# The first half of the node update by plain float32 matmuls on the weights as loaded

## What is computed

```python
h = maximum(layernorm(x), 0)
# layer 0: three kinds of edges (hh, oo, ho), logits from gathered rows
feat = concatenate([h[src], h[dst]], axis=1)
logit = relu(feat @ W_kind + b_kind) @ W_a + b_a
alpha = softmax of logit over the edges of one dst
z = segment_sum(alpha * h[src], dst)
nf2 = concatenate([h, z], axis=1)             # 512 x 2048
h_new = relu(nf2[:128] @ W_hn + b_hn)          # node update
o_new = relu(nf2[128:] @ W_on + b_on)
x = x + concatenate([h_new, o_new])
# layer 1
x = x + normalized_adjacency @ (maximum(layernorm(x), 0) @ W.T + b)
```

## Time and profile before

| | |
|---|---|
| times of 3 runs | 653.9, 653.91, 651.59 us, median 653.9 |
| profiled execution | 651.15 us, span 649.0 us, mean granted clock 0.939 |
| PE, PEld | 556.4 us (86%), 412.9 us (64%) |
| DVE, ACT, POOL | 454.9 us (70%), 307.4 us (47%), 176.3 us (27%) |
| DMA | 140.51 MB, mean 216 GB/s |
| chain that ended last | PE 57%, DVE 20%, DMA 11%, ACT 6% |

### The profile page before, as it was taken

One profiled execution on the slowest core, in us unless ns is written; L12 is line 12 of the kernel. 1 busy time (PEld: TensorE's weight loads), 2 busy tenths in 40 slices (PEclk: granted clock), 3 DMA queues, 4 the chain that ended last, 5 costly groups with the idle time before them and its releaser, 6 DMA issues.

```text
span 649.0 us, 8205 instructions
## 1 busy us (share of the span) xinstructions
PE 556.4 (86%) x2376; PEld 412.9 (64%) x2377; DVE 454.9 (70%) x958; ACT 307.4 (47%) x485; POOL 176.3 (27%) x165
## 2 busy tenths in 40 slices
PE   0799999999839998959899997558949999779987
PEld 0688777777617776647576775224738778667865
DVE  6715256786985879988989887486795289783252
ACT  2623312214088996556565755399743182322200
POOL 2000300165464664555647642200030000000000
PEclk9999999999968999989889999688968899979999
DMA  8334453499999999999999997943355075121021
GB/s 330 122 135 163 151 202 124 144 259 380 316 308 356 330 343 325 303 321 333 284 361 327 349 348 262 232 136 103 127 213 208 16 249 198 41 88 42 0 82 48
DMA packets 55973, 140.51 MB, mean 216 GB/s; under 512 B 6274, under 2 KB 6402, under 8 KB 55938
## 3 DMA queue, kind: packets, MB, share of 16 engines
q0 software_dynamic: 20624, 74.98, 37.5%
q1 hardware_dynamic: 27072, 50.34, 22.0%
q10 hardware_dynamic: 8242, 14.75, 6.1%
HBM read 123.27 MB, written 16.78 MB: 216 GB/s over the span
## 4 chain that ended last, share of the span: by engine, by line
PE 57%; DVE 20%; DMA 11%; ACT 6%; issue 4%; POOL 1%; ACTq 0%; DVEq 0%; POOLq 0%
PE ps L638 35%; DMA gath<-tab_b,tabl_i 8%; PE ps L624 6%; PE ps L588 5%; DVE gath L893 4%; PE ps L797 3%; ACT onehot L482 3%; PE ps L769 3%; DVE ring_l L868 2%; PE ps L782 2%; DVE gath L888 2%; DMA gath<-tab_a,tabl_i 2%; DVE onehot L910 2%; DVE logit_d L932 1%; DVE logit_d L1021 1%
## 5 line engine op out<-in xcount | busy, mean ns | idle before, releaser
L638 PE MATMUL ps<-ring_h,actT_h 128*128 128x512 f32 x520 | 226.0, 435 | 28.2 <-ACT stage L453 16.4
L638 PE MATMUL ps<-ring_h,actT_l 128*128 128x512 f32 x520 | 206.4, 397 | 0.0
L638 PE MATMUL ps<-ring_l,actT_h 128*128 128x512 f32 x520 | 206.2, 397 | 0.0
L435 ACT CAST ring_h<-raw 128x512 fp32r<-128x512 f32 x176 | 105.0, 616 | 118.4 <-PE ps L638 82.8
L482 ACT ACTIVATE onehot<-onehot,lgs 128x512 bf16<-128x512 bf16 x192 | 124.6, 712 | 69.4 <-DVE onehot L910 55.3
L868 DVE TENSOR_TENSOR ring_l<-raw,ring_h 128x512 fp32r<-128x512 f32 x176 | 116.8, 685 | 43.2 <-ACT ring_h L435 42.9
L638 PEld LDWEIGHTS ps<-ring_h,actT_h 128*128 128x128 f32 x520 | 99.9, 192 | 60.8 <-ACT stage L453 18.3
L638 PEld LDWEIGHTS ps<-ring_h,actT_l 128*128 128x128 f32 x520 | 99.7, 192 | 22.4
L638 PEld LDWEIGHTS ps<-ring_l,actT_h 128*128 128x128 f32 x520 | 100.0, 192 | 20.3
L293 POOL DMA_INDIRECT gath<-tab_a,tabl_i x64 | 71.0, 1109 | 150.2 <-DVE gath L893 77.0
L588 PE MATMUL ps<-onehot 128*128 128x512 bf16 x292 | 83.8, 397 | 20.8 <-ACT onehot L482 17.8
(11 more groups left out here) (162 smaller groups left out, 505.1 us busy)
## 6 DMA issues: line engine op xcount, KB each, us to landing
raw<-in_L_gnn_W_ho_dram SPq DMA_DIRECT2D x32, 256.0 KB
raw<-in_L_gnn_W_oo_dram SPq DMA_DIRECT2D x32, 256.0 KB
raw<-in_L_gnn_W_hh_dram SPq DMA_DIRECT2D x32, 256.0 KB
raw<-in_L_gnn_W_on_dram SPq DMA_DIRECT2D x32, 256.0 KB
raw<-in_L_gnn_W_hn_dram SPq DMA_DIRECT2D x32, 256.0 KB
tab_a<-stage ACTq DMA_DIRECT2D x24, 256.0 KB
tab_b<-stage ACTq DMA_DIRECT2D x24, 256.0 KB
raw<-in_L_gnn_W_dram SPq DMA_DIRECT2D x16, 256.0 KB
```

Of the source, the lines that this page charges most:

```text
L435: nc.scalar.copy(ring_h[:, k, :], raw[:, k % RAW, :]).then_inc(s_high, 1)
L638: mm = nc.tensor.matmul(ps[:, first + m, :], w, v, start=(k == 0 and i == 0), stop=(k == KT - 1 and i == 2))
```

## The change

In chunks 12 to 15 PE no longer takes the three float32r passes. It runs one plain float32 matmul for each block and step, with `actT` as weights and `raw[k]` as loaded (`node_chunk`). So ACT has no `round_w` and DVE no `low_w` for these 32 steps. `actT` is the sum of the two parts of `h`; DVE writes it over `actT_l`, slice j at its place (11, j+2), after PE has finished step (11,j), the last reader of that slice of `actT_l`. A slice of `raw` is free for the next load only when PE has read it: the loads of chunks 13 to 16 wait for PE's step one chunk earlier, where they waited for DVE's `low_w`. The counters of later chunks are renumbered by `nth_split`.

```diff
+        actT = sb("actT", [P, KT, N], F32, over="actT_l")
...
                 for k in range(KT):
+                    if q == CH_EDGE:
+                        sp.wait_ge(s_low, q * KT + k + 1)
+                    elif q <= CH_NODE:
+                        sp.wait_ge(s_slot, KT + (q - 1) * KT + k + 1)
+                    else:
+                        sp.wait_ge(s_low, nth_split(q) * KT + k + 1)
                     load(w, row, n, q, k)
...
-                    if q * KT + k + AHEAD < (CH_EDGE + 4) * KT:
+                    if q * KT + k + AHEAD < CH_EDGE * KT:
                         rounds(q * KT + k + AHEAD, q * KT + k + AHEAD + 1)
...
+            def node_chunk(q, ms, bank_free, before):
+
+                for k in range(KT):
+                    before(k)
+                    pe.wait_ge(s_raw[k], 16 * q + 16)
+                    pe.wait_ge(s_whole, k + 1)
+                    for m in ms:
+                        if k == 0 and bank_free:
+                            bank_free(m)
+                        mm = nc.tensor.matmul(ps[:, NM + m, :], actT[:, k, m * P:(m + 1) * P], raw[:, k, :], start=(k == 0), stop=(k == KT - 1))
+                    mm.then_inc(s_slot, 1)
...
-                chunk(q + c, NM, ms, free, before=lambda k: last_sums(q + c, k))
+                node_chunk(q + c, ms, free, before=lambda k: last_sums(q + c, k))
...
-                    if q1 < CH_EDGE + 4:
+                    if q1 < CH_EDGE:
                         low_w(q1, k1)
...
+                    j = (q - CH_EDGE + 1) * KT + k - 2
+                    if 0 <= j < KT:
+                        dve.wait_ge(s_slot, KT + (CH_EDGE - 1) * KT + j + 1)
+                        nc.vector.tensor_tensor(actT[:, j, :], f32(actT_h[:, j, :]), f32(actT_l[:, j, :]), ALU.add).then_inc(s_whole, 1)
```

More of the change, by code:

```diff
@@ L162, in gnn_kernel @@
         s_h = sem("h_rows")
+        s_whole = sem("h_whole")
         s_norm = sem("h_normed")
@@ L209, in gnn_kernel, with nth_split @@
         CH_EDGE = 3 * 2 * NN
+        CH_NODE = CH_EDGE + 4
+        def nth_split(q):
+            return q - 4
         hn, on = (W_hn, (0,)), (W_on, (1, 2, 3))
@@ L229, in load @@
             def load(w, row, n, q, k):
-                sp.wait_ge(s_low, q * KT + k + 1)
                 sp.dma_start(raw[:, k % RAW, :], w[bass.ds(row + k * P, P), n * FB:(n + 1) * FB]).then_inc(s_raw[k % RAW], 16)
@@ L237, in _ @@
                         for k in range(KT):
+                            sp.wait_ge(s_low, ((half * NN + n) + t * 2 * NN) * KT + k + 1)
                             load(w, half * D, n, (half * NN + n) + t * 2 * NN, k)
@@ L631, in chunk @@
                         before(k)
-                    pe.wait_ge(s_low, RAW + q * KT + k + 1)
+                    pe.wait_ge(s_low, RAW + (q if counted else nth_split(q)) * KT + k + 1)
                     for m in ms:
@@ L765, in _ @@
                 for k in range(KT):
-                    pe.wait_ge(s_low, RAW + q * KT + k + 1)
+                    pe.wait_ge(s_low, RAW + nth_split(q) * KT + k + 1)
                     for i, (w, v) in enumerate(passes(actT_h[:, k, m * P:(m + 1) * P], actT_l[:, k, m * P:(m + 1) * P],
@@ L793, in _ @@
                 for k in range(KT):
-                    pe.wait_ge(s_low, RAW + (q + 1) * KT + k + 1)
+                    pe.wait_ge(s_low, RAW + nth_split(q + 1) * KT + k + 1)
                     for i, (w, v) in enumerate(passes(actT_h[:, k, m * P:(m + 1) * P], actT_l[:, k, m * P:(m + 1) * P],
@@ L866, in low_w @@
             def low_w(q, k):
-                dve.wait_ge(s_high, q * KT + k + 1)
+                dve.wait_ge(s_high, (q if q < CH_EDGE else nth_split(q)) * KT + k + 1)
                 nc.vector.tensor_tensor(ring_l[:, k, :], raw[:, k % RAW, :], f32(ring_h[:, k, :]), ALU.subtract).then_inc(s_low, 1)
```

## The result

The changed kernel takes 657.67 us (median of 20 runs), the kernel before 654.51 (20 runs of the same series). The ratio is 1.0051, with a 95% interval from 1.0032 to 1.0071: slower by 0.5%, 3.3 us. The forecast was 653.6, in a range from 647 to 660, with "within 0.5%" as the likeliest case. The time is in the range and lies at the 0.5% bound, on the slower side. The profiled run took 656.02 us, span 653.9.

The account below looks back on a forecast made before the run. The bound changes: DMA and PE, then waits for gathers and the table store, ACT from 423 us, DVE from 457. +2 - 3.4 + 2.5 = +1.1 us gives 652.3, or 655.0 from the median; forecast 653.6, range 647 to 660.

Parts of the forecast that it names:

- The price of a float32 matmul: Chunks 12 to 15 on PE: 0.92 us per float32 product against 0.69 for three passes, 0.23 us more.
- The two streams' rival: Faster: a float32 matmul is two streams, 0.46 us; sum -7.1 us, 644 (from the median 647); chance 0.1.
- Part A: Up to the second kind's end (416 us): DVE's waits delay the table store 5.1 us, partly made up; +2 us.
- Its own sign of being wrong: Tile 62's gather before 401 or after 407 us; also records at 0.23 us, or PE waiting in chunk 11.
- The lockstep: Slower: DVE's waiting for PE costs in full; +5.2 us, 656.4 (from the median 659); slower by over 0.5%: 0.33.
- The moved loads: Faster: eight loads leave the gathers' way, store lands 4 us earlier; sum -4.9, 646.3; all faster cases together 0.25.
- Chunk 12 hidden: Chunk 12 costs PE 5.5 us more, hidden by PE's 9.3 us of idle time before 419.5 us.
- Part B: From the second kind's end to chunk 15: ACT's casts and a DVE `low_w` go; -3.4 us, between -4.1 and -2.
- Part C: Chunk 15 to attention product: DVE saves four `low_w`, but ACT's copy waits for PE's longer chunk 15; +2.5 us.
- the base: Starting time for the sum: profiled execution's 651.15 us or the three-run median, 2.75 higher; forecast took the middle.

Follow-up runs that it names:

- the wait alone: Kernel before with only DVE's eight waits for PE's steps of chunk 11 added, no sums: 659.78 us, ratio 1.0074.
- copy and store earlier: Changed kernel with DVE's copy of the last table ahead of the last sum and ACT's store at k = 1: 647.46 us, ratio 0.9904.
- the casts put back: Changed kernel with sums at j+5, plus 32 idle ACT casts at the old places of chunks 12 to 15: 648.04 us, ratio 0.9935.
- the late sums: Changed kernel with each sum and its wait three places later in DVE's queue, j+5 instead of j+2: 645.23 us, ratio 0.9869.

## Why the prediction was right or wrong

**The price of a float32 matmul: right in kind, its excess over the three passes a third too high.** The page's group of the new matmuls and the group of their weight loads:

```profile
L672 PE MATMUL ps<-raw,actT 128*128 128x512 f32 x128 | 63.5, 633 | 6.7 <-DVE stage L901 4.3
L672 PEld LDWEIGHTS ps<-raw,actT 128*128 128x128 f32 x128 | 25.8, 204 | 32.4 <-issue 29.2
```

128 records for 64 matmuls, two each, as forecast; 42 of them take 18.04 us in the chain, 0.43 each, where I had 0.46. A matmul is 0.86 us and costs 0.17 more than its three passes, not 0.23. Chunk 15 is so 4.1 us longer, not 5.5. The two streams' rival is out. That a record streams the moving operand twice, as I had argued, no row shows: it shows two records of 0.43 us, 1.9 times 0.23.

**Part A: this is the step that failed.** I had put +2 there, from "The bytes before the store's end are nearly the same, and the DMA engines were full, so part of the 5.1 us is made up". It measured +5.4. The lag of the store was worked out nearly rightly (5.1 us; 391.94 - 381.26 = 10.7 us behind chunk 11 against 385.68 - 379.73 = 6.0, so 4.7). What failed is the inference from full engines. They were full only as long as DVE freed gather slots in time. POOL issues gathers as DVE frees slots, and a DVE held to PE's pace frees them late (5.56, 4.53 and 2.89 us of waiting in POOL's rows), so the engines stand partly idle and have the bytes left to move. The five profiles with DVE's wait at j+2 have a share of 0.58 to 0.63 from 21 to 14 us ahead of the end of chunk 11, the nine others 0.99 to 1.03. With the wait alone the share falls to 0.84 from 351 to 366 us, and the 5.0 us of lag come through to tile 62's gather as 6.1, although the share is 0.98 beside the store. In the changed kernel it falls to 0.84 there and to 0.85 between 381 and 392 us as well. Nor was the store's whole way a transfer: before, the share from 399 to 403 us, ahead of the gather that waited for it, is 0.34. The prediction had the fact in its hands ("gathers were issued late themselves") and used it only as relief for the store. Its own sign of being wrong came true: the gather of tile 62 starts at 410.02, after 407.

Two of its rivals were real. The lockstep measured by itself is +4.8 us (it put 5.1 on A, and 1 more if PE waited); its sum, 656.4 or 659 from the median, is the one that holds the measured 657.7. The moved loads by themselves are -4.2 (it said -4 for A, of which the profiles show 1.9). I had let them nearly cancel. They do not simply add in the changed kernel: there the wait costs 11.9 us (sums at j+2 against j+5), of which, by the estimate above, some 9 depend on where the store stands; 1.7 are in B. Why it is more than double stays open. The share of 0.98 between 381 and 392 us with the early loads and of 0.85 without them suggests that the loads used to fill the time in which DVE held the gathers back, and now come later beside the store. A kernel before with the wait and the moved loads together would tell the two apart; there is none here.

**Chunk 12 hidden: right.** It is 4.1 us longer and PE waited 4.34 us for its banks besides, a wait that I had not named. Taking it away (copy and store earlier) brought nothing that shows.

**Part B: right.** -3.4 forecast, -3.3 measured. ACT's 21 parts follow each other in 12.97 us, 0.62 each with no cast between, and ran from 429.55 to the copy at 442.52, 13.0 us, before 16.0. With the casts put back it is 16.1.

**Part C: right in mechanism, over-sized.** +2.5 forecast, +1.3 measured; with 0.17 for 0.23 in 24 matmuls the forecast would have been +1.1. What is late next is ACT behind PE, as said: the chain goes from 42 records of L672 through the copies to L554. Moving the copy takes 1.1 us off C in the profile.

**Sum.** +1.1 forecast, +3.4 by the three stretches (+3.3 by the ratio); the difference is A's +3.4 less C's 1.2. The rest of the 4.1 us between 653.6 and 657.7 is the base: I stood between two, and the longer series of the kernel before (654.5) bears out the upper one. That middle also put the forecast 0.3 us under the median of 653.9 that was known then, while the sum said slower. That 657.7 lies in the range owes something to its width: the two bounds of A alone span 6 us.

The idea itself pays: with its sums out of DVE's way the conversion-free node update is 8.6 us faster than the kernel before. If the parts add, 4.2 of that are the moved loads and about 6.8 the conversions (ratio 0.9973 less 0.9869), and what remains, +2.4, is the price of the float32 matmuls and the sums. That is an estimate: loads and wait did not add.

## What to carry to other kernels

Before you call a queue saturated, ask who issues its transfers and whether the change delays that engine: a share of 1.04 is the outcome of an order of work, not a property of the stretch. An engine that runs ahead of the one that bounds the kernel is doing something with its lead; work that must wait for the bounding engine belongs as far behind as its reader allows, since three places in a queue were worth 12 us here. And where a queue waits for one transfer (11.45 us before tile 62's gather), look first for what stands between that transfer's data and its issue: the place of one issue in ACT's queue cost 6 us in one kernel and 12 in the other.

## What the runs showed of the hardware

A float32 matmul of 128x128 by 128x512 is two records of 0.43 us each at the full granted clock, so 0.86 us against 0.69 for the three float32r passes (0.23 each). The Trainium skill ("FP8 and Floating Point Precision", TensorE Precision Notes) speaks of four passes; the trace has two records, whose sum is 3.7 times a float32r pass.

PE's clock was lower behind idle time. Between 381 and 392 us, where PE worked 6.66 of 11 us, the granted clock was 0.69 on average; behind the wait for ACT at 440 us the first pair of float32 records took 2.01 us and the next 1.00, and from 448 us on 0.86 (PE's rows of the chain):

```profile
443.13 2.01 PE ps L672 x2
445.14 1.28 PE ps L601 x3
446.42 1.00 PE ps L672 x2
447.43 0.65 PE ps L601 x3
```

The three one-hot sums took 1.28 us and then 0.65, twice the rate: these are the two levels, 1.2 and 2.4 GHz. In B that is 1.15 + 0.14 + 0.63 = 1.9 us. With the late sums the first pair took 1.10 us and everything behind it the full rate, and B was 1.7 us shorter (25.3).
